# Expert results scattered to token order during the block loop instead of gathered after it, and an attention's first group put ahead of the second batch's rows

## The chip, the cores and the metric

The kernel runs on one core of a Trainium2 chip. Its time is the device time of one execution in microseconds. Engines are named as in the profile: PE (TensorE, matrix products; PEld its weight loads), DVE (VectorE), ACT (ScalarE), POOL (GpSimd), SP (SyncE, which here only issues DMAs; its issues are shown as SPq).

## What is computed

A decoder of four layers on `x` of 4 batches x 512 tokens x 128 features (16 heads), with a context of 77 positions. Every layer is an attention, then a feed-forward part, each with a normalization before and an addition to `x` after.

- Layer 0: causal self-attention with small convolutions, then a mixture of 8 experts (hidden 512, GELU, two experts a token) plus a shared expert.
- Layer 1: attention that samples the context at 5 computed offsets per head, then a mixture of 8 experts with a SiLU gate (hidden 352, two experts a token).
- Layer 2: plain cross attention, then a mixture of 8 experts (hidden 512, ReLU, two experts a token).
- Layer 3: plain cross attention, then product keys: 8192 single-row experts, one chosen per head.

The part that the change touches is the mixture. In the reference:

```python
# layer 0 and 2: every expert, weighted by a gate that is zero but for two experts
for e in range(N_EXPERTS):
    h = act(xf @ Wfc[e] + bfc[e]) @ Wproj[e] + bproj[e]
    routed = routed + h * gate[:, e:e + 1]
# layer 1: rows already multiplied by their gate value and sorted by expert
for e in range(num_experts):
    h = silu(xe @ w1[e]) * (xe @ w3[e])
    out = out + h @ w2[e] * m
```

## The kernel before

**Tiling.** The 2048 tokens are 16 tiles of 128 rows (`NTT`), 4 of them (`NT`) to a batch. `x_all` stays in SBUF for the whole kernel. The kernel is written engine by engine: each stage is a block in which every engine has an own instruction list, and semaphores set what waits for what. So the order on an engine is the order in which the functions of its list are called.

**Stages.** `first_causal` is layer 0's attention and the routing for the first mixture, to about 640 us. Then three times `expert_stage(n)`: the mixture of layer n, and behind it on every engine the attention of layer n+1. Stage 0 is from 640 (sampled attention from 742), stage 1 from 1094 (cross attention from 1194), stage 2 from 1449 (cross attention from 1543, then `product_keys`). The mixture with n == 1 is called `gated`.

**Routing.** Per batch, `normed` (DVE, L649) writes the normalized rows of its four tiles, one operation of 128x128 each. Then logits, the choice of two experts (`pick`) and the number of tokens ahead (`places`) give each row two slots, `slot_i`. `scatter` (POOL, L762) sends each tile's rows twice by indirect DMA to the DRAM array `xs_d`, which is ordered by expert. In the gated layer the rows are multiplied by their two gate values first (`scaled` is the second set of rows).

**Block loop.** The slots are cut into `NBLK` = 23 blocks of `BLK` = 256 rows, each of one expert. For block i: SP loads its rows (L778) into one of three buffers `xb`; PE turns them (`turn`, L956, counted by `m_T`); ACT copies the turned rows out (L1019); PE multiplies up (L974, or L967 and L969 for the two halves of the gated hidden layer); ACT applies the function (L1031 or L1029); in the gated layer DVE multiplies the halves (`gate_hidden`, L877); PE multiplies down (L983, `m_down`); DVE moves the result with its bias to one of two buffers `yb` (`result`, L888, gated L886, counted by `m_y`); SP stores it to `ys_d` (L784), in slot order. DVE also copies the weights of block i+3 (`weights`, L867 to L869, gated L860 to L863). PE's order is `up(i)`, `down(i-1)`, `turn(i+2)`. DVE's order is `gate_hidden(i+1)` (gated only), `result(i)`, `weights(i+3)`. SP's order is `load(i+3)`, `store(i)`.

**Behind the loop.** POOL gathers with two indirect DMAs per tile (L810) the two results of each token from `ys_d`, into four buffers, and waits for the addition of four tiles before. DVE adds them to `x_all` (`combine`; L919 in the gated layer, 128x128 twice a tile; L921 with the gate value otherwise), then computes the attention's statistics (L2525, L2528, in the sampled attention L3096), POOL makes the reciprocal deviations (`rstd`, L2196, L2197), and DVE the normed rows (L2536). In a cross attention PE then turns them (L2264), makes queries (L2270, L2276), products for the rows' maxima (`max_scores`, L2289; DVE's `maxima`, L2543), turns the maxima (L2297; DVE adds them as `maximum_in`, L2557), and per group of four query tiles scores (L2309), exponentials on ACT (L2449) and weighted sums (L2322). The groups are the loop `for G in range(G4)`.

After the loop of stage 1 SP also loads the third mixture's weights (`load_wide`, L212 to L215).

## Time and profile before

| | us |
|---|---|
| three runs | 1899.67, 1910.25, 1910.5 (median 1910.25) |
| profiled execution, its own time | 1902.02 |
| its span | 1900.3 |
| PE busy | 1273.0 (67%) |
| DVE busy | 1026.5 (54%) |
| POOL busy | 565.7 (30%) |
| ACT busy | 530.6 (28%) |

The span is the time from the first to the last recorded instruction; the rest of the execution's time lies around it. The busy shares are means over stages that have different limits, so the views by stage below say more than the table.

### The profile page before, as it was taken

To read this page: it belongs to the slowest core of one execution; us is meant where nothing else is said; L and a number is where in the kernel's file an instruction comes from. 1 tells how busy PE (TensorE), PEld (TensorE's weight loads), DVE (VectorE), ACT (ScalarE), POOL (GpSimd) and SP (SyncE) were. 2 spreads that over 40 slices of the span, in tenths; PEclk is the share of its full clock that TensorE was granted. 3 is DMA by queue.
4 is the path that set the end of the run, shared out by engine and by line. 5 is a ranking of instruction groups with operands and counts; after the bars stand their busy time and mean duration, and the time that the engine had idled before them with its cause. 6 is when DMAs were issued, how large, how long until landed. Compare 5 with 4: busy or idle time off the path is not lost. (4 is left out here: it accounts for less than half of the span.)

```text
span 1900.3 us, 26101 instructions
## 1 busy us (share of the span) xinstructions
PE 1273.0 (67%) x9212; PEld 771.8 (41%) x9212; DVE 1026.5 (54%) x2918; ACT 530.6 (28%) x1053; POOL 565.7 (30%) x700
## 2 busy tenths in 40 slices
PE   1458878787884896455645399378876955787720
PEld 1223334343442785345645288222335842222210
DVE  2454455454553232599999655334433325547796
ACT  0123233332341452122312133023423522323310
POOL 6041222212334002541011600331132033155674
PEclk8588798887995998555555599669967978866665
DMA  5930000000003121433532111400001210022232
GB/s 135 389 136 1 1 1 1 1 1 0 12 7 105 41 67 48 119 100 92 136 93 61 34 60 62 130 23 1 12 18 49 67 49 23 2 63 64 79 98 74
DMA packets 73254, 116.48 MB, mean 61 GB/s; under 512 B 11565, under 2 KB 52320, under 8 KB 70624
## 3 DMA queue, kind: packets, MB, share of 16 engines
q1 hardware_dynamic: 60320, 85.24, 14.9%
q0 software_dynamic: 12800, 29.51, 5.4%
q8 instruction: 76, 1.25, 0.3%
q14 instruction: 58, 0.48, 0.1%
HBM read 77.03 MB, written 37.68 MB: 60 GB/s over the span
## 5 line engine op out<-in xcount | busy, mean ns | idle before, releaser
L1671 DVE CUSTOM_DVE_ANT_0 arena<-ps,far 128x512 f32<-128x512 f32 (+3 forms) x256 | 118.2, 488 | 108.6 <-PE ps L1345 107.7
L2002 POOL DMA_INDIRECT wide<-in_w_ud,arena x128 | 130.0, 1015 | 77.7 <-DVE arena L2033 40.7
L2922 PE MATMUL ps<-wide,arena 78*128 78x32 bf16 x3840 | 112.1, 187 | 51.6 <-ACT wide L3035 41.8
L1260 POOL TENSOR_SCALAR_AFFINE_SELECT arena<-arena 128x260 f32<-128x260 f32 (+1 forms) x128 | 53.7, 432 | 308.9 <-ACT arena L1538 308.8
L810 POOL DMA_INDIRECT arena<-ys_d,slot_i x64 | 61.2, 956 | 246.6 <-DMA ys_d<-arena 197.4
L2922 PEld LDWEIGHTS ps<-wide,arena 78*128 78x128 bf16 x3840 | 110.3, 104 | 58.9 <-ACT wide L3035 45.2
L983 PEld LDWEIGHTS ps<-arena 128*128 128x128 f32 (+1 forms) x1012 | 123.4, 192 | 4.0
L983 PE MATMUL ps<-arena 128*128 128x128 f32 (+1 forms) x1012 | 123.6, 275 | 0.0
L1538 ACT ACTIVATE arena<-ps 128x1024 f32<-128x1024 f32 (+1 forms) x96 | 84.6, 881 | 109.9 <-PE ps L1367 109.4
L1367 PE MATMUL ps<-arena 32*128 32x128 f32 (+3 forms) x512 | 114.2, 491 | 1.1 <-DVE arena L1690 1.1
L2543 DVE TENSOR_REDUCE arena<-ps 128x6 f32<-128x462 f32 (+1 forms) x96 | 54.9, 581 | 93.6 <-PE ps L2289 69.9
L1345 PE MATMUL ps<-fr 32*128 32x256 f32 (+3 forms) x256 | 91.2, 433 | 19.7 <-DVE arena L1671 18.1
L1379 PE MATMUL ps<-arena 128*9 128x128 f32 (+3 forms) x512 | 91.7, 460 | 4.2 <-POOL arena L1260 4.1
L1318 PE MATMUL ps<-arena,wq_rows 128*128 128x512 f32 x96 | 71.9, 910 | 33.5 <-issue 32.5
L2449 ACT ACTIVATE arena<-ps 77x1024 f32<-77x1024 f32 x64 | 65.2, 1019 | 92.7 <-PE ps L2309 75.0
L974 PE MATMUL ps<-arena 128*128 128x256 f32 x368 | 88.6, 384 | 1.6 <-DVE arena L869 1.6
L2322 PE MATMUL ps<-arena 77*9 77x512 f32 x256 | 84.0, 741 | 0.0
L1031 ACT ACTIVATE arena<-ps,arena 128x256 f32<-128x256 f32 x184 | 75.6, 470 | 28.9 <-PE ps L974 28.8
L2309 PE MATMUL ps<-arena 32*77 32x512 f32 x256 | 80.0, 705 | 5.2 <-DVE arena L2557 2.8
L888 DVE TENSOR_TENSOR arena<-ps,b_rows 128x256 f32<-128x256 f32 x46 | 19.5, 424 | 117.9 <-PE ps L983 117.9
L810 POOL DMA_INDIRECT b_rows<-ys_d,slot_i x32 | 38.3, 1198 | 136.4 <-DMA ys_d<-arena 127.3
L1345 PEld LDWEIGHTS ps<-fr 32*128 32x128 f32 x256 | 41.7, 190 | 83.8 <-DVE arena L1671 49.6
(498 smaller groups left out, 2632.4 us busy)
## 6 DMA issues: line engine op xcount, KB each, us to landing
arena<-low_d SPq DMA_DIRECT2D x32, 780.0 KB
xs_d<-zrow SPq DMA_DIRECT2D x1, 10240.0 KB, 30.1
ys_d<-zrow SPq DMA_DIRECT2D x1, 10240.0 KB, 55.9
arena<-xs_d SPq DMA_DIRECT2D x69, 128.0 KB, 2.0
ys_d<-arena SPq DMA_DIRECT2D x69, 128.0 KB, 1.7
arena<-in_w SPq DMA_DIRECT2D x2, 1408.0 KB
wide<-in_Wfc SPq DMA_DIRECT2D x1, 2048.0 KB, 11.8
wide<-in_Wproj SPq DMA_DIRECT2D x8, 256.0 KB, 6.5
```

Of the source, the lines that this page charges most:

```text
L810: pool.indirect_dma_start(out=yg[:, t % 4, j, :], out_offset=None, in_=ys_d, in_offset=bass.IndirectOffsetOnAxis(ap=slot_i[:, j, t:t + 1], ...
L974: nc.tensor.matmul(ps[:, 1 + i % 2 * 2 + c // 2, c % 2 * BLK:c % 2 * BLK + BLK], w1s[:, i % 3, lo:lo + w], xT[:, i % 2, :], start=True, st ...
L983: mm = nc.tensor.matmul(ps[:, 5 + i % 2, t * P:t * P + P], hT[0:w, i % 2, c, t * P:t * P + P], w2s[0:w, i % 3, c, :], start=c == 0, stop=c ...
L1345: mm = nc.tensor.matmul(ps[:, n % 2, 384 * i:384 * i + P * t + P], q3r[rows, G % 2, P * t:P * t + P], kcr[rows, G % 2, 0:P * t + P], start ...
L1367: mm = nc.tensor.matmul(ps[:, 2 + n % 2 * 2 + i, o:o + T - P * kt], kc[rows, G % 3, P * kt:P * kt + P], q3[rows, G % 3, P * kt:T], start=T ...
L1379: mm = nc.tensor.matmul(ps[32 * r:32 * r + HD + 1, 6, P * kt:T], v9[:, G // 4 % 3, kt, 4 * (G % 4) + r, :], pt[:, n // 3 % 2, i, COL[kt]:C ...
L1538: nc.scalar.activation(pt[:, n // 3 % 2, :, o:o + w], ps[:, 2 + n % 2 * 2:4 + n % 2 * 2, 0:w], ACT.Exp, scale=SCALE)\
L1671: ins = nc.vector.tensor_tensor_reduce(junk[:, n % 2, 384 * i:384 * i + w], ps[:, n % 2, 384 * i:384 * i + w], far[:, T - w:T], 1.0, 3 * N ...
L2002: pool.indirect_dma_start(out=rows_g[t % 4][:, h, :], out_offset=None, in_=A["w_ud"], in_offset=bass.IndirectOffsetOnAxis(ap=eidi[:, t % 8 ...
L2309: mm = nc.tensor.matmul(ps[0:S2, 2 + n % 2 * 2 + j, :], kS[rows, G % 4, G // 4, :], q3[rows, G % 3, :], start=True, stop=True)
L2322: mm = nc.tensor.matmul(ps[32 * r:32 * r + HD + 1, 6, :], v9[:, G // 4, 4 * (G % 4) + r, :], pt[:, n % 3, j, :], start=True, stop=True)
L2922: mm = nc.tensor.matmul(ps[:, 2 * (i % 3) + h // 2, col:col + 4 * HD], ring[m_ % 4][:, h * NK + p_, t % 2 * P:t % 2 * P + P], table[n // 4 ...
```

## The change

1. **Rows carry their destination.** `xs_d` gets a 129th column. `normed` writes into it, as a float, the row number in a new array `y_d` where this row's result belongs: token order, one half for first choices and one for second choices. Since a row's two copies now differ, the layers without gates write a second full set of normed rows (`twins`): four operations of 128x128 and two small ones more per batch. In the gated layer `scaled` becomes `twins`, with two small operations more per batch.
2. **Results go to token order.** SP no longer stores. `result(i)` on DVE first computes `goal`, the two addresses of each partition, from column 128 of `xb`, and POOL sends each block's result with two indirect DMAs to `y_d` (`results`). Padding rows go to rows of their own (`trash`).
3. **A load waits for one thing more.** `load(i)` waits not only for the turn of block i-3 but also for `goal` of block i-3, and all loads follow one another on SP.
4. **No gathers.** After the loop SP loads plain rows, two DMAs of 256 KB a batch (`summands`; the last batch's in `last_rows`, with the third mixture's weights behind it in stage 1). `combine` is two additions of 128x512 in the gated layer; in the others still eight operations.
5. **Cross attentions begin in another order.** `maximum_rows(0)`, `queries(2)`, the scores and first weighted sum of group 0 and `maximum_rows(1)` stand ahead of the second batch's rows (`normed(1)`, `rounded_queries(1)`); the loop starts at G = 1.
6. The zero fill of `ys_d` is gone; `load_gated` waits for two scatters.

The core of the diff:

```diff
                 last_user = max((j for j in range(b) if rows[j] is rows[b]), default=-1)
                 if last_user >= 0:
                     dve.wait_ge(scattered[last_user], 32 * NT * (n + 1))
+                nc.vector.tensor_scalar(rows[b][:, :, D], token[:, tiles(b)], float(STAGE * n + NTT * P), None, ALU.add)
+                if not gated:
+                    nc.vector.tensor_scalar(twins[b][:, :, D], token[:, tiles(b)], float(STAGE * n), None, ALU.add)
+                    for t in range(NT):
+                        nc.vector.tensor_scalar(twins[b][:, t, 0:D], xa[:, NT * b + t, :], mv16[:, NT * b + t, 0:1],
+                                                rstd16[:, NT * b + t:NT * b + t + 1], ALU.subtract, ALU.mult)
                 for t in range(NT):
-                    nc.vector.tensor_scalar(rows[b][:, t, :], xa[:, NT * b + t, :], mv16[:, NT * b + t, 0:1],
+                    nc.vector.tensor_scalar(rows[b][:, t, 0:D], xa[:, NT * b + t, :], mv16[:, NT * b + t, 0:1],
                                             rstd16[:, NT * b + t:NT * b + t + 1], ALU.subtract, ALU.mult).then_inc(r["xn"], 1)
...
                     g = lambda j: gval[:, j, ts].unsqueeze(2).to_broadcast([P, NT, D])
-                    nc.vector.tensor_tensor(scaled[b][:, :, :], rows[b][:, :, :], g(0), ALU.mult).then_inc(r["scaled"], 1)
+                    nc.vector.tensor_scalar(twins[b][:, :, D], token[:, ts], float(STAGE * n), None, ALU.add)
+                    nc.vector.tensor_tensor(twins[b][:, :, 0:D], rows[b][:, :, 0:D], g(0), ALU.mult).then_inc(r["scaled"], 1)
                     dve.wait_ge(r["scaled"], 2 * b + 1)
-                    nc.vector.tensor_tensor(rows[b][:, :, :], rows[b][:, :, :], g(1), ALU.mult).then_inc(r["scaled"], 1)
...
+            sent = lambda p, count: 32 * (n * len(range(p, NBLK, 2)) + count)
 
             def sync(sp):
                 def load(i):
                     r = sp.value_load(bmap[0:1, 1, i:i + 1], min_val=0, max_val=SLOTS - BLK)
                     if i >= 3:
                         sp.wait_ge(m["T"], i - 2)
+                        sp.wait_ge(m["goal"], i - 2)
                     sp.dma_start(xb[:, i % 3, :, :], xs_d[bass.ds(r, BLK), :].rearrange("(p c) d -> p c d", c=2))\
                         .then_inc(m[f"x{i % 3}"], 16)
 
-                def store(i):
-                    r = sp.value_load(bmap[0:1, 1, i:i + 1], min_val=0, max_val=SLOTS - BLK)
-                    sp.wait_ge(m["y"], i + 1)
-                    sp.dma_start(ys_d[bass.ds(r, BLK), :].rearrange("(p c) d -> p c d", c=2), yb[:, i % 2, :, :])\
-                        .then_inc(m[f"ys{i % 2}"], 16)
-
                 if n == 0:
+                    for b in (1, 2):
+                        sp.wait_ge(scattered[b], 32 * NT)
                     load_gated(sp)
...
                 sp.wait_ge(m["bmap"], 1)
                 for b in range(B):
                     sp.wait_ge(scattered[b], 32 * NT * (n + 1))
-                for i in range(3):
+                for i in range(NBLK):
                     load(i)
-                for i in range(NBLK):
-                    if i + 3 < NBLK:
-                        load(i + 3)
-                    store(i)
+                settled(sp)
+                for b in range(B - 1):
+                    summands(sp, b)
+
+            def summands(sp, b):
+                if b >= 2:
+                    sp.wait_ge(m["added"], b - 1)
+                for j in range(2):
+                    lo = TRASH + NTT * P * j + T * b
+                    sp.dma_start(yg[b % 2][j], y_d[lo:lo + T, :].rearrange("(t p) d -> p t d", p=P)).then_inc(m[f"ys{b % 2}"], 16)
+
+            def last_rows(sp):
+                summands(sp, B - 1)
                 if n == 1:
                     load_wide(sp, "ffn2", "W1", "W2", "b2")
 
-
-            def gpsimd(pool, rows, scaled):
-                scatter(pool, n, B - 1, rows, scaled)
-
-            def gather(pool, lo, hi):
-                for t in range(lo, hi):
-                    if t >= 4:
-                        pool.wait_ge(m["added"], t - 3)
-                    for j in range(2):
-                        pool.indirect_dma_start(out=yg[:, t % 4, j, :], out_offset=None, in_=ys_d,
-                                                in_offset=bass.IndirectOffsetOnAxis(ap=slot_i[:, j, t:t + 1], axis=0))\
-                            .then_inc(gathered[t % 4], 16)
+            def gpsimd(pool, rows, twins):
+                scatter(pool, n, B - 1, rows, twins)
+
+            def results(pool):
+                for i in range(NBLK):
+                    pool.wait_ge(m["y"], i + 1)
+                    for c in range(2):
+                        pool.indirect_dma_start(out=y_d, in_=yb[:, i % 2, c, :], in_offset=None,
+                                                out_offset=bass.IndirectOffsetOnAxis(ap=goal[:, i % 2, c:c + 1], axis=0))\
+                            .then_inc(landed[i % 2], 16)
 
             def settled(eng):
-                for b in range(2):
-                    eng.wait_ge(m[f"ys{b}"], 16 * len(range(b, NBLK, 2)))
+                for p in range(2):
+                    eng.wait_ge(landed[p], sent(p, len(range(p, NBLK, 2))))
...
                 def result(i, one):
+                    if i >= 2:
+                        dve.wait_ge(landed[i % 2], sent(i % 2, i // 2))
+                    dve.wait_ge(m[f"x{i % 3}"], 16 * (i // 3 + 1))
+                    nc.vector.scalar_tensor_tensor(goal[:, i % 2, :], xb[:, i % 3, :, D], float(-STAGE * n), trash[:, i, :], ALU.add, ALU.max).then_inc(m["goal"], 1)
                     dve.wait_ge(m["down"], i + 1)
-                    if i >= 2:
-                        dve.wait_ge(m[f"ys{i % 2}"], 16 * (i // 2))
                     y = ps[:, 5 + i % 2, 0:BLK].rearrange("p (c d) -> p c d", c=2)
...
             def combine(dve, ch, b):
-                for t in range(NT * b, NT * b + NT):
-                    added_to(dve, ch, t)
-
-            def added_to(dve, ch, t):
-                dve.wait_ge(gathered[t % 4], 32 * (NTT // 4 * n + t // 4 + 1))
+                dve.wait_ge(m[f"ys{b % 2}"], 32 * (b // 2 + 1))
                 for j in range(2):
                     if gated:
-                        ins = nc.vector.tensor_tensor(xa[:, t, :], xa[:, t, :], yg[:, t % 4, j, :], ALU.add)
+                        ins = nc.vector.tensor_tensor(x_all[:, b, :, :], x_all[:, b, :, :], yg[b % 2][j], ALU.add)
                     else:
-                        ins = nc.vector.scalar_tensor_tensor(xa[:, t, :], yg[:, t % 4, j, :], gval[:, j, t:t + 1], xa[:, t, :],
-                                                             ALU.mult, ALU.add)
+                        for t in range(NT):
+                            ins = nc.vector.scalar_tensor_tensor(x_all[:, b, t, :], yg[b % 2][j][:, t, :], gval[:, j, NT * b + t:NT * b + t + 1],
+                                                                 x_all[:, b, t, :], ALU.mult, ALU.add)
                     if j == 0:
...
+                    blocks.results(pool)
...
                 max_scores(0, 0, 12)
+                maximum_rows(0)
+                queries(2)
+                scores(0, 0)
+                scores(0, 1)
+                weighted(0)
+                maximum_rows(1)
                 normed(1)
                 rounded_queries(1)
-                maximum_rows(0)
-                for G in range(G4):
+                max_scores(1, 0, 4)
+                for G in range(1, G4):
                     nb = G // 4 + 1
                     top = lambda n: max_scores(nb, 4 * (G % 4) + n, 4 * (G % 4) + n + 1) if nb < B and G % 4 < 3 else None
                     top(0)
...
                 maxima(0, 0, 12)
                 maximum_out(0)
+                maximum_in(0)
+                maximum_out(1)
                 norms(1)
+                maximum_in(1)
                 normed(1)
-                maximum_in(0)
-                for G in range(G4):
+                maxima(1, 0, 4)
+                for G in range(1, G4):
                     nb = G // 4 + 1
                     more = nb < B and G % 4 < 3
```

DVE in the loop of the gated layer, before. L877 is `gate_hidden` of the next block, L886 the result, L860 to L863 the weight copies.

```order
L877 TENSOR_TENSOR arena<-arena,ps 128x256 [waits m_act] x2
L877 TENSOR_TENSOR arena<-arena,ps 96x256 [waits m_act]
L886 COPY arena<-ps 128x256 [waits m_ys0,m_down]
L855 TENSOR_LOAD bmap
L855 ISA x2
L860 ISA [waits m_down]
L860 COPY arena<-arena 128x352
L861 ISA
L861 COPY arena<-arena 128x352
L862 ISA
L862 COPY arena<-arena 128x256
L863 ISA
```

The same place now. L902 is `gate_hidden`, L909 the new address operation, L913 the result.

```order
L902 TENSOR_TENSOR arena<-arena,ps 128x256 [waits m_act] x2
L902 TENSOR_TENSOR arena<-arena,ps 96x256 [waits m_act]
L909 SCALAR_TENSOR_TENSOR goal<-arena,trash 128x2 [waits m_x2,landed1]
L913 COPY arena<-ps 128x256 [waits m_down]
L880 TENSOR_LOAD bmap
L880 ISA x2
L885 ISA [waits m_down]
L885 COPY arena<-arena 128x352
L886 ISA
L886 COPY arena<-arena 128x352
L887 ISA
L887 COPY arena<-arena 128x256
```

The address operation of a block has come between the gate products of the next block and the result.

SP in the loop of a mixture, before. L778 is the load of a block, L784 the store of a result, L775 and L782 the reading of the block's address.

```order
L775 TENSOR_LOAD bmap
L775 ISA x2
L778 ISA [waits m_T]
L778 DMA arena<-xs_d 128x256
L782 TENSOR_LOAD bmap
L782 ISA x2
L784 ISA [waits m_y]
L784 DMA ys_d<-arena 128x256
```

The same place now. L800 is the load.

```order
L800 DMA arena<-xs_d 128x258
L796 TENSOR_LOAD bmap
L796 ISA x2
L800 ISA [waits m_goal,m_T]
L800 DMA arena<-xs_d 128x258
```

The stores are gone, and each load waits for `m_goal` beside `m_T`.

DVE at the start of the cross attention of stage 1, before. L2551 belongs to the first batch's maxima, L919 are additions of the second batch's results, L2525 to L2536 its statistics and rows, L2557 the maxima's way in for the first group.

```order
L2551 TENSOR_SCALAR arena<-arena 128x16 [waits c_max]
L919 TENSOR_TENSOR x_all<-x_all,arena 128x128 [waits gathered0]
L919 TENSOR_TENSOR x_all<-x_all,arena 128x128 [waits dve_chain]
...
L2525 BN_STATS arena<-x_all 128x6 [waits m_added]
L2525 BN_STATS arena<-x_all 128x6 x3
L2528 BN_AGGR arena<-arena 128x2 [waits c_stats]
L2528 BN_AGGR arena<-arena 128x2 x3
L2536 TENSOR_SCALAR arena<-x_all,arena 128x128 [waits turn7,c_rstd,c_mean]
L2536 TENSOR_SCALAR arena<-x_all,arena 128x128 x3
L2557 TENSOR_TENSOR arena<-arena,ps 128x512 [waits free7_act,turn7]
```

The same place now. L2583 is `maximum_out`, L2589 `maximum_in`, L942 the additions, L2557 to L2568 statistics and rows.

```order
L2583 TENSOR_SCALAR arena<-arena 128x16 [waits c_max]
L2589 TENSOR_TENSOR arena<-arena,ps 128x512 [waits free7_act,turn7]
L2583 TENSOR_SCALAR arena<-arena 128x16 [waits turn7,c_max]
L942 TENSOR_TENSOR x_all<-x_all,arena 128x512 [waits m_ys1]
L942 TENSOR_TENSOR x_all<-x_all,arena 128x512 [waits dve_chain]
L2557 BN_STATS arena<-x_all 128x6 [waits m_added]
L2557 BN_STATS arena<-x_all 128x6 x3
L2560 BN_AGGR arena<-arena 128x2 [waits c_stats]
L2560 BN_AGGR arena<-arena 128x2 x3
L2589 TENSOR_TENSOR arena<-arena,ps 128x512 [waits free7_act,turn7]
L2568 TENSOR_SCALAR arena<-x_all,arena 128x128 [waits turn7,c_rstd,c_mean]
L2568 TENSOR_SCALAR arena<-x_all,arena 128x128 x3
```

The first group's L2589 has moved ahead of the additions and rows of the second batch, and the additions are two.

## Rows read from the trace of the kernel before

**Rows 1.** Busy time by window: PE, PEld, DVE, ACT, POOL, PE clock, DMA
```profile
860.00:1055.00 195.00, 106.28 (x2948) 100.56 (x2946) 185.18 (x340) 45.87 (x137) 34.08 (x27) 0.53 0.36 92
...
1094.00:1194.00 100.00, 98.26 (x598) 87.10 (x598) 56.01 (x172) 36.09 (x93) 0.06 (x1) 0.98 0.19 59
...
1306.00:1316.00 10.00, 6.59 (x30) 2.43 (x28) 7.82 (x33) 3.21 (x4) 1.79 (x4) 1.00 0.00 0
```

**Rows 2.** Timeline of the gated loop: start, duration, operation, idle before
```profile
1158.16 0.38 PE L956 MATMUL ps<-ident,arena 128*128 128x128 f32 x2
...
1161.59 0.42 DVE L877 TENSOR_TENSOR arena<-arena,ps 96x256 f32<-96x256 f32 x1 [0.44 <-ACT arena L1029]
...
1162.31 0.38 PE L956 MATMUL ps<-ident,arena 128*128 128x128 f32 x2
```

**Rows 3.** Timeline of stage 0's loop: PE, DVE and SP
```profile
714.61 0.44 PE L956 MATMUL ps<-ident,arena 128*128 128x128 f32 x2
...
718.71 0.42 DVE L888 TENSOR_TENSOR arena<-ps,b_rows 128x256 f32<-128x256 f32 x1 [2.02 <-PE ps L983]
...
719.31 0.36 SPq L784 DMA_DIRECT2D ys_d<-arena  x1
...
719.96 0.42 DVE L869 COPY arena<-wide 128x512 f32 x1
...
720.42 0.33 SPq L778 DMA_DIRECT2D arena<-xs_d  x1
...
722.45 0.44 PE L956 MATMUL ps<-ident,arena 128*128 128x128 f32 x2
```

**Rows 4.** Timeline, VectorE: normed rows, a small operation
```profile
1417.65 1.20 DVE L649 TENSOR_SCALAR arena<-x_all,mv,rstd 128x128 f32<-128x128 f32 x4 [0.56 <-POOL rstd L640]
...
1229.24 0.18 DVE L2551 TENSOR_SCALAR arena<-arena 128x16 f32<-128x16 f32 x1
```

**Rows 5.** Timeline around indirect DMAs of POOL, and SP's first loads
```profile
1443.71 1.05 POOL L762 DMA_INDIRECT xs_d<-arena,slot_i  x1 [0.30 <-issue]
...
1443.84 0.42 DVE L869 COPY arena<-wide 128x512 f32 x1
...
1446.84 3.65 SPq L778 DMA_DIRECT2D arena<-xs_d  x4
...
817.90 2.15 POOL L810 DMA_INDIRECT b_rows<-ys_d,slot_i  x1 [0.30 <-issue]
```

**Rows 6.** Timeline, ends of the gated and third loops; one DMA group; VectorE addition
```profile
1191.88 0.42 DVE L886 COPY arena<-ps 128x256 f32<-128x256 f32 x1 [0.51 <-PE ps L983]
...
1193.22 0.42 DVE L886 COPY arena<-ps 128x256 f32<-128x256 f32 x1 [0.91 <-PE ps L983]
...
1194.68 12.88 SPq L214 DMA_DIRECT2D wide<-in_W  x8
...
1211.60 0.87 DVE L2525 BATCH_NORM_STATS2 arena<-x_all 128x6 f32<-128x128 f32 x4
...
1542.33 0.43 DVE L888 TENSOR_TENSOR arena<-ps,b_rows 128x256 f32<-128x256 f32 x1 [1.36 <-PE ps L983]
...
1557.09 0.87 DVE L2525 BATCH_NORM_STATS2 arena<-x_all 128x6 f32<-128x128 f32 x4
...
ws<-in_Wproj_s SPq DMA_DIRECT2D x1, 256.0 KB, 4.0
...
1249.20 0.69 DVE L2557 TENSOR_TENSOR arena<-arena,ps 128x512 f32<-128x512 f32 x1 [0.22 <-PE ps L2297]
```

**Rows 7.** Timeline, VectorE: waits behind gathers of later batches
```profile
1274.00 2.99 DVE L2536 TENSOR_SCALAR arena<-x_all,arena 128x128 f32<-128x128 f32 x4 [7.48 <-POOL arena L2197]
...
807.08 0.74 DVE L921 SCALAR_TENSOR_TENSOR x_all<-b_rows,gval,x_all 128x128 f32<-128x128 f32 x2 [4.72 <-DMA b_rows<-ys_d,slot_i]
```

**Rows 8.** Timeline, stage 1's second batch: VectorE additions, TensorE turning rows
```profile
1229.33 2.19 DVE L919 TENSOR_TENSOR x_all<-x_all,arena 128x128 f32<-128x128 f32 x8
...
1234.89 1.23 PE L2264 MATMUL ps<-ident,arena 128*128 128x128 f32 x4 [6.20 <-DVE arena L2536]
```

168 lines of the change are left out of this document (89 added, 79 removed).

## Prediction

> **What bounds the kernel now.** I read the engines' busy time by stage first (the windows), then the timeline of one block in each kind of mixture stage, then the ends of the block loops and the first microseconds of the attentions behind them. The windows say that the three block loops are TensorE's: 98.26 us of matmul in the 100 us from 1094, at a granted clock of 0.98, while the sampled attention from 860 is VectorE's, 185.18 of 195 us [rows 1]. So inside a block loop any wait that TensorE gets is paid in full, and it is paid 20 times over; at the joints between loop and attention, what counts is who comes last. Three places decide the change: the loop of the gated stage, the routing of the rows, and the joints.
>
> **The gated loop (the new wait).** A block's life before: TensorE turns block i (L956) at 1158.16, then multiplies block i-1 up and starts block i-2's down, and turns the next block at 1162.31, a period of 4.15 us [rows 2]. VectorE's last gate product of block i-1 (L877) starts at 1161.59 and takes 0.42, so it ends 3.85 us behind the turn. Before, the load of block i+1 asked only for the turn that had emptied its buffer, three blocks back, and came early. Now it also asks for the address words (`goal`) of block i-2, since these are read from column 128 of the same buffer. On VectorE `goal(i-2)` stands behind the gate products of block i-1 (the first two listings of the change), and these need TensorE's up products of i-1, which stand behind the turn of block i. So each turn now waits for a load that waits for gates that wait for the turn before: one closed ring, whose length is turn to gates 3.85, the address operation 0.2 (the small operation of [rows 4] takes 0.18), from VectorE's end to SyncE's issue 0.18 (copy-out of the other stages: starts 718.71, lasts 0.42, store issued 719.31 [rows 3]), and the load itself 2.03 (issued 720.42, turn at 722.45 in the rows where the turn comes right behind it [rows 3]). The sum is 6.26; with SyncE's small jitter I write 6.28. Against 4.15 that is 2.13 us more, and blocks 3 to 22 have such a load: 20 x 2.13 = **+42.6 us**. The register reads of SyncE (0.75 between two of its issues: 719.31 + 0.36 to 720.42) are done while it waits, and are not in the ring. Nothing hides this: TensorE is what fills the loop. Behind SyncE's wait only the next loads are queued, and TensorE alone waits for those.
>
> **The two loops without gates.** There `goal(i-3)` stands on VectorE behind the result of block i-4 and the weight copies that follow it, with no gates between. The ring is over two blocks: result (L888) at 718.71, end of the last copy 719.96 + 0.42 = 720.38, so 1.67; then 0.2, 0.18 and 2.03, which is 4.08 to the turn; from a turn to the result two products on, 718.71 - 714.61 = 4.10 [rows 3]. Together 8.18, where two blocks now take 722.45 - 714.61 = 7.84. That is 0.17 a block, x 20 x 2 stages = **+6.8**. The first few may have slack, so the bounds are 0 and 10.
>
> **The routing of rows.** `normed` writes in the layers without gates a second set of rows (`twins`): four operations of 128x128, 1.20 us as a group, and two of 128x4, some 0.17 each by the nearest small one [rows 4]: 1.5 per batch. Before the first mixture all four batches lie on VectorE's path or close to it, before the third three to four; take 4 and 3: 10.5. The gated layer gets the two small ones alone, 4 x 0.35 = 1.4. **+11.9**; where VectorE waits for GpSimd's rstd anyway (0.56 before this group) a part may vanish, so 5 to 14.
>
> **Results sent by GpSimd.** Two indirect DMAs per block in place of one store by SyncE. GpSimd is idle during the loops, and an indirect DMA of 128 rows takes it 1.05 with 0.30 between two [rows 5]: 2.7 per block, under the shortest period of 3.9, and landed (1.3 us behind the last: SyncE's first load at 1446.84 less the 0.75 register reads less 1444.76 [rows 5]) before the result two blocks on. Nothing is charged while that holds.
>
> **Joint at the end of a loop.** Gated, before: last results start at 1191.88 and 1193.22, SyncE then issues eight wide loads (12.88 us, 1.6 each), the gathers of the first batch run beside them, and the first batch's statistics start at 1211.60 [rows 6]. Now: the last two pairs by GpSimd from 1192.4, 4 x 1.35 less a gap ends at 1197.5; landed 1198.8; SyncE's two plain loads of 256 KB 0.2 later, 4.0 for the first (a lone one of that size [rows 6]) and 1.6 for the second: 1204.6; two additions of 128x512 at 0.69 [rows 6] behind 0.2: 1206.2. A gain of **5.4**. In the loops without gates, before: last result at 1542.33, statistics at 1557.09 [rows 6]. Now: the last pair starts at 1543.8 (the pair before it holds GpSimd until then) and ends 2.4 later, then 1.3, 0.2, 5.6, 0.2 as above and eight additions of 0.37 (0.74 for two, the operation of the 807.08 row [rows 7]), 3.0: 1556.5. A gain of 0.6 each, **1.2**. The zero fill of the old result array is not on the path and counts nothing.
>
> **Joints between batches.** The gathers of the second half stand on GpSimd ahead of the third batch's rstd; VectorE waits 7.48 us there (1274.00), and the next stage repeats the pattern; in the sampled attention the adds themselves wait 4.72 (807.08) [rows 7]. With plain loads issued early by SyncE these go: 7.0 + 7.0 + 4.7 = **18.7**. Late next is then GpSimd's rstd itself, for which I leave the remainder. Two additions for eight in the gated combine: 2.19 [rows 8] to 1.4; one batch of the three stands on the path, **0.8**.
>
> **The first group ahead of the second batch's rows.** TensorE stands 6.20 us before 1234.89, waiting for the rows of batch 1 [rows 8]. The change puts maximum rows, queries and scores of that group into this hole. Scores need ScalarE's exponentials behind them, and batch 1's rows come later by them, so I grant 2.5 us of the 6.2 in the first such attention and 1.0 in the second, where VectorE's eight additions stay: **3.5**, with bounds from -2 to 6.
>
> **Sum.** 42.6 + 6.8 + 11.9 = 61.3 lost; 5.4 + 1.2 + 18.7 + 0.8 + 3.5 = 29.6 won; net +31.7. The profiled execution took 1902.0 us (span 1900.3), so 1933.7 on its scale; by the median of the runs shown, 1910.25, 1942. Three runs are at 1910.25, 1910.5 and 1899.67; the profiled one lies low among them, and I predict between the two, **1938**.
>
> **Rivals.**
> A. The clock. With 4.15 us of matmul in 6.28, TensorE would be busy for 66% of the gated loop. The sampled attention shows 106.28 of 195 us busy at a clock of 0.53; against it, ten microseconds at 6.59 busy from 1306 had 1.00 [rows 1]. If it falls to the lower level (1.2 GHz), the part of the ring that is matmul, some 2.8 us, doubles: 20 x 2.8 = 56 more, 1993. 10%.
> B. GpSimd's scatters are held up, and the wait for landed results takes over as the ring. For it: one indirect DMA took 2.15 (817.90) beside long VectorE operations; against it, 1.05 beside the copies of the block's weights, 0.42 at 1443.84 [rows 5]. Two of 2.15 are 4.3, 0.34 above the period without gates; x 40 = 14 more, 1951. 8%.
> The Trainium skill ("SBUF — State Buffer", section "SBUF: two separate sides", its warning on VectorE and DMA) says that a DMA issued by GpSimd stalls while VectorE copies fp32 within SBUF, since both want one port pair; the weight copies of each block are of that kind. By that rule each pair of scatters would grow by up to the block's copies, 1.0 to 1.2 us, which alone would still fit into either period. The trace speaks against even that much: the 1.05 row stands beside such copies.
> C. The other side: the gated load's wait is hidden, because the address operation comes a block earlier than I read. Then +42.6 falls away: 1938 - 43 = 1895, about 1885 with a bigger gain at the joints, which is faster. It decides where the load lands before TensorE is ready to turn, so where `goal` ends 2.2 us (issue and landing) ahead of the turn. The gates end at 1162.01, only 0.30 ahead of the turn at 1162.31 [rows 2], so it takes a `goal` of one block before, whose gates ended 4.15 earlier. The order speaks against it. 10%, for what I may have misread there.
> D. The gains at the joints don't come, since GpSimd's rstd, or the first loads, are late instead: only 10 of 29.6. 1938 + 20 = 1958. 7%.
>
> **How the numbers follow.** Forecast 65%, own range 1920 to 1955 (routing 5 to 14, gateless loops 0 to 10, first group -2 to 6, plus the two scales 8 apart). The range reaches over B and D, and a little down: **1915 to 1958**; outside lie A and C, 20%. One per cent (1891 to 1929) is about what a measurement of this kernel can tell from no change. Faster: half of C and a trace of the forecast, 0.06; same: the other half of C and the low end of the forecast, 0.10; slower: 0.84.
>
> **What would show it.** In the profile of the changed kernel: a period of 6.3 us between turns in the gated loop, TensorE idle some 2 us before each turn with the load as its releaser, and the loop about 43 us longer; 4.1 in the other two; each load issued 0.2 behind a `goal`; no 7 us wait before the third batch's normed rows; the clock still near 1 in the gated loop. I am wrong if the load of block i+1 is seen to be issued before the gates of block i-1 end, if the clock there is near 0.5, or if the scatters of a block take longer than its period.

## The result, and the profile after

The changed kernel takes 1961.72 us (median of four runs, 1957.04 to 1965.78), the kernel before 1904.97 (1899.67 to 1910.5): a ratio of 1.0297, with an interval of 1.0247 to 1.0346. It is 57 us slower. The forecast was slower too, by 32 us: 1938, with a range to 1958, and the time lies 4 us above that range. The profiled executions have spans of 1900.3 and 1955.3, so there are 55.0 us to be found between the two traces.

To find them I cut both timelines at the same nine events: first turn of each block loop, last result of it, first statistics of the attention behind it. The three of the gated stage in the changed kernel, in rows like those in [rows 2] and [rows 6] (start, duration, operation, idle before):

```profile
1103.98 0.66 PE L980 MATMUL ps<-ident,arena 128*128 128x128 f32 x2 [4.67 <-DMA arena<-xs_d]
...
1254.11 0.43 DVE L913 COPY arena<-ps 128x256 f32<-128x256 f32 x1 [0.85 <-PE ps L1007]
...
1264.65 0.87 DVE L2557 BATCH_NORM_STATS2 arena<-x_all 128x6 f32<-128x128 f32 x4
```

All stretches, each from the event before to the one named:

| stretch, to | before | after | difference | forecast |
|---|---|---|---|---|
| first turn of stage 0 | 647.0 | 660.4 | +13.4 | +6.0 |
| last result of stage 0 | 93.0 | 98.0 | +4.9 | +3.4 |
| first statistics behind it | 14.6 | 13.1 | -1.6 | -0.6 |
| first turn of stage 1 (sampled attention) | 339.3 | 332.5 | -6.8 | -3.3 |
| last result of stage 1 (gated loop) | 99.3 | 150.1 | +50.9 | +42.6 |
| first statistics | 18.4 | 10.5 | -7.8 | -5.4 |
| first turn of stage 2 (cross attention) | 237.4 | 237.2 | -0.2 | -5.8 |
| last result of stage 2 | 93.3 | 97.9 | +4.6 | +3.4 |
| first statistics | 14.8 | 11.1 | -3.7 | -0.6 |
| end (cross attention, product keys) | 343.2 | 344.5 | +1.3 | -8.0 |
| sum | 1900.3 | 1955.3 | +55.0 | +31.7 |

**The ring is there.** Two blocks of the gated loop after, where [rows 2] had a turn every 4.15 us (a row of PE L980 is a turn, L902 is the gate product, L909 the addresses):

```profile
1162.36 0.44 PE L980 MATMUL ps<-ident,arena 128*128 128x128 f32 x2 [1.91 <-DMA arena<-xs_d]
...
1165.84 0.42 DVE L902 TENSOR_TENSOR arena<-arena,ps 96x256 f32<-96x256 f32 x1 [0.44 <-ACT arena L1053]
1166.17 0.15 DVE L909 SCALAR_TENSOR_TENSOR goal<-arena,trash 128x2 int32<-128x2 f32 x1
...
1168.51 0.44 PE L980 MATMUL ps<-ident,arena 128*128 128x128 f32 x2 [1.79 <-DMA arena<-xs_d]
1168.73 0.96 POOL L835 DMA_INDIRECT y_d<-arena,goal  x1 [0.30 <-issue]
1168.78 0.89 PE L991 MATMUL ps<-arena 128*128 128x256 f32 x2
1169.47 1.06 PE L993 MATMUL ps<-arena 128*128 128x256 f32 x2
```

TensorE now stands idle before each turn, 1.8 to 2.0 us (once 2.2), and it is the load that releases it. From turn to gate end to addresses to the next turn are 6.15 us, where 6.28 had been worked out. But look at the last two rows: the same pair of up products that took 0.59 us now takes 0.89 and 1.06. The next turn comes at 1176.45, 7.94 behind. Of the 20 periods with a waiting load, 14 are 6.1 to 6.3 and six are 7.8 to 8.3. The granted clock falls to 0.5 in this loop six times, for 3.41 us each, and the six long periods are those.

**The joints are shorter**, and by more than forecast. The end of the gated loop, to compare with [rows 6]:

```profile
1253.47 0.96 POOL L835 DMA_INDIRECT y_d<-arena,goal  x1 [1.71 <-DVE arena L913]
...
1257.27 0.96 POOL L835 DMA_INDIRECT y_d<-arena,goal  x1 [0.30 <-issue]
1259.53 6.03 SPq L821 DMA_DIRECT2D arena<-y_d  x6
1263.20 1.42 DVE L942 TENSOR_TENSOR x_all<-x_all,arena 128x512 f32<-128x512 f32 x2 [8.66 <-DMA arena<-y_d]
```

Between SyncE's first load and the additions lie 3.7 us; I had 5.8 for them, made of 4.0 for a lone transfer, 1.6 for the second and 0.2 behind it. The 4.0 of [rows 6] isn't a lone transfer's: it was issued 0.47 us behind another of 256 KB, in a row of loads issued one behind the other:

```profile
36.54 0.43 SPq L233 DMA_DIRECT2D ws<-in_Wfc_s  x1
37.01 0.43 SPq L233 DMA_DIRECT2D ws<-in_Wproj_s  x1
```

The first of these took 3.6 us to land, the second 4.0, so both were there 4.5 us behind the first issue. The company was in that figure already, and the 1.6 charged it once more.

**The clock in the last cross attention** is the third thing to see. Windows of 20 us from the first statistics of stage 2 (length, busy PE, PEld, DVE, ACT, POOL with the number of instructions, PE clock, DMA share and GB/s):

```profile
1610.80:1630.80 20.00, 13.17 (x28) 6.00 (x28) 10.88 (x31) 2.35 (x4) 2.53 (x3) 0.67 0.09 26
1630.80:1650.80 20.00, 13.56 (x34) 4.42 (x33) 7.62 (x24) 4.28 (x6) 2.53 (x3) 0.59 0.09 27
1650.80:1670.80 20.00, 17.16 (x46) 5.14 (x44) 8.61 (x29) 5.84 (x7) 1.29 (x3) 0.67 0.00 0
1670.80:1690.80 20.00, 16.80 (x38) 4.79 (x39) 4.79 (x9) 4.38 (x6) 3.46 (x2) 0.50 0.00 1
```

TensorE is busy for 16.80 of 20 us in the last of them, and gets little done: 38 products, since it runs at 1.2 GHz throughout.

### The profile page after: what moved, and what is told of

The parts are those of the page before. It is cut to its first block and busy times, and to the rows that moved or that the text cites. A ratio compares the mean times of both kernels' runs of the same rounds, so it can differ in the third digit from the quotient of the medians.

```text
span 1955.3 us, 25917 instructions
## 1 busy us (share of the span) xinstructions
PE 1326.0 (68%) x9212; PEld 788.1 (40%) x9212; DVE 1049.0 (54%) x3019; ACT 531.6 (27%) x1053; POOL 599.5 (31%) x744
## 5 line engine op out<-in xcount | busy, mean ns | idle before, releaser
L835 POOL DMA_INDIRECT y_d<-arena,goal x138 | 133.0, 964 | 255.5 <-DVE arena L915 130.9
L2953 PE MATMUL ps<-wide,arena 78*128 78x32 bf16 x3840 | 109.9, 187 | 50.0 <-ACT wide L3066 41.5
L1392 PE MATMUL ps<-arena 32*128 32x128 f32 (+3 forms) x512 | 121.0, 522 | 1.2 <-DVE arena L1715 1.2
L1370 PE MATMUL ps<-fr 32*128 32x256 f32 (+3 forms) x256 | 92.4, 439 | 18.1 <-DVE arena L1696 16.5
L1404 PE MATMUL ps<-arena 128*9 128x128 f32 (+3 forms) x512 | 99.0, 492 | 1.4 <-POOL arena L1285 1.4
L1343 PE MATMUL ps<-arena,wq_rows 128*128 128x512 f32 x96 | 70.0, 888 | 31.7 <-issue 30.7
L2349 PE MATMUL ps<-arena 77*9 77x512 f32 x256 | 89.0, 782 | 2.2 <-ACT arena L2479 2.2
L2336 PE MATMUL ps<-arena 32*77 32x512 f32 x256 | 86.1, 787 | 4.9 <-DVE arena L2589 4.9
L980 PE MATMUL ps<-ident,arena 128*128 128x128 f32 x138 | 30.8, 308 | 62.7 <-DMA arena<-xs_d 60.9
## 6 DMA issues: line engine op xcount, KB each, us to landing
wide<-in_Wfc SPq DMA_DIRECT2D x1, 2048.0 KB, 11.1
```

Of the source, the lines that this page charges most:

```text
L835: pool.indirect_dma_start(out=y_d, in_=yb[:, i % 2, c, :], in_offset=None, out_offset=bass.IndirectOffsetOnAxis(ap=goal[:, i % 2, c:c + 1] ...
L1370: mm = nc.tensor.matmul(ps[:, n % 2, 384 * i:384 * i + P * t + P], q3r[rows, G % 2, P * t:P * t + P], kcr[rows, G % 2, 0:P * t + P], start ...
L1392: mm = nc.tensor.matmul(ps[:, 2 + n % 2 * 2 + i, o:o + T - P * kt], kc[rows, G % 3, P * kt:P * kt + P], q3[rows, G % 3, P * kt:T], start=T ...
L1404: mm = nc.tensor.matmul(ps[32 * r:32 * r + HD + 1, 6, P * kt:T], v9[:, G // 4 % 3, kt, 4 * (G % 4) + r, :], pt[:, n // 3 % 2, i, COL[kt]:C ...
L2336: mm = nc.tensor.matmul(ps[0:S2, 2 + n % 2 * 2 + j, :], kS[rows, G % 4, G // 4, :], q3[rows, G % 3, :], start=True, stop=True)
L2349: mm = nc.tensor.matmul(ps[32 * r:32 * r + HD + 1, 6, :], v9[:, G // 4, 4 * (G % 4) + r, :], pt[:, n % 3, j, :], start=True, stop=True)
```

## The experiments

The questions were: is the gated loop the ring of load and gates, and what are its six long periods; why does the start cost 13.4; and why do the two cross attentions give back nothing. All ratios below are to the kernel before, run on the same chip.

**e1: addresses one block earlier.** Four address buffers, and the operation ahead of the gate products:

```diff
+                def address(i):
+                    if i >= 4:
+                        dve.wait_ge(landed[i % 2], sent(i % 2, i // 2 - 1))
+                    dve.wait_ge(m[f"x{i % 3}"], 16 * (i // 3 + 1))
+                    nc.vector.scalar_tensor_tensor(goal[:, i % 4, :], ...)
+
                 def result(i, one):
+                    dve.wait_ge(m["down"], i + 1)
                     if i >= 2:
                         dve.wait_ge(landed[i % 2], sent(i % 2, i // 2))
-                    dve.wait_ge(m[f"x{i % 3}"], 16 * (i // 3 + 1))
-                    nc.vector.scalar_tensor_tensor(goal[:, i % 2, :], ...)
-                    dve.wait_ge(m["down"], i + 1)
...
+                address(0)
...
                 for i in range(NBLK):
+                    if i + 1 < NBLK:
+                        address(i + 1)
                     if gated and i + 1 < NBLK:
                         gate_hidden(i + 1)
```

> The changed kernel with four address buffers, and the addresses of block i+1 computed ahead of the gate products of block i+1 (one block earlier than now), everything else as changed. Ring theory: the load of a block no longer stands behind the gates, turns in the gated loop come every 4.15 to 4.3 us with no longer one in between, the first turn to the last result takes 100 us where it now takes 150, and the loops without gates win some 4 us each: 1961.7 - 51 - 8 = about 1903. Rival, that the 23 pairs of indirect DMAs (or the wait for what they have landed) hold the loops: periods stay above 5 us and the time above 1940.

Measured: 1879.18 us (1875.57 to 1880.14), ratio 0.9855 (0.9833 to 0.9877). The gated loop takes 98.5 us (150.1 in the changed kernel, 99.3 before); its periods, but for the first two, are 4.14 to 4.16. Two turns a block apart, and between them the address operation, now well ahead of the load that asks for it:

```profile
1143.77 0.39 PE L987 MATMUL ps<-ident,arena 128*128 128x128 f32 x2
...
1145.78 0.15 DVE L909 SCALAR_TENSOR_TENSOR goal<-arena,trash 128x2 int32<-128x2 f32 x1
...
1147.92 0.38 PE L987 MATMUL ps<-ident,arena 128*128 128x128 f32 x2
```

So the ring was the cause of the loop's growth, and the 23 pairs of scatters are no bound. The whole kernel came out 24 us better than I expected. The loops without gates are the largest part of that: 88.0 and 89.0 us where I expected 94. Their period is 3.73 from the fourth at the latest, which is shorter than before the change (93.0; pairs like 3.79 and 4.2).

**e2: the old order of the cross attentions**, on all engines, with everything else as changed. TensorE's part:

```diff
                 max_scores(0, 0, 12)
-                maximum_rows(0)
-                queries(2)
-                scores(0, 0)
-                scores(0, 1)
-                weighted(0)
-                maximum_rows(1)
                 normed(1)
                 rounded_queries(1)
-                max_scores(1, 0, 4)
-                for G in range(1, G4):
+                maximum_rows(0)
+                for G in range(G4):
```

> The changed kernel with both cross attentions in the order of before (first group behind the second batch's rows). As predicted (the new order wins 3.5 us): 1965. Rival, that the new order costs, since the first group's products run before TensorE's clock has risen and push the second batch's rows back: 1952 to 1958, and the third batch's normed rows start at or under 59 us behind the first statistics of stage 1, where the changed kernel has 60.8.

Measured: 1943.83 us (1941.9 to 1946.12), ratio 1.0199 (1.0177 to 1.022): 18 us less than the changed kernel, more than the rival had said. It is not in stage 1 (236.9 against 237.2; the third batch's normed rows start 60.3 behind the first statistics, not under 59) but in the last stretch: 330.4 against 344.5. The windows that answer to those above:

```profile
1611.50:1631.50 20.00, 10.70 (x22) 4.75 (x22) 12.10 (x36) 2.34 (x4) 2.53 (x3) 0.67 0.09 26
1631.50:1651.50 20.00, 14.56 (x46) 5.76 (x47) 7.23 (x22) 5.99 (x8) 2.53 (x3) 0.77 0.09 27
1651.50:1671.50 20.00, 14.54 (x53) 5.49 (x53) 11.78 (x34) 4.82 (x6) 4.75 (x4) 0.83 0.00 0
1671.50:1691.50 20.00, 18.11 (x73) 5.76 (x73) 6.55 (x15) 9.20 (x12) 0.00 (x0) 1.00 0.00 1
```

With the new order TensorE does more in the first 20 us (28 products against 22), as intended. From then on its clock is lower: 0.59, 0.67, 0.50 against 0.77, 0.83, 1.00, and after 80 us the old order has done 194 products to the new one's 146.

**e3 and e7: idle products in the wait.** 12, then 8 products of 128x128 that nobody reads, on TensorE ahead of each turn in the gated loop.

```diff
+                    if gated and i and i + 2 < NBLK:
+                        pe.wait_ge(m["xT"], i + 1)
+                        for _ in range(12):
+                            nc.tensor.matmul(ps[:, 7 * (i % 2), 3 * P:4 * P], ident[:, :], ident[:, :], start=True, stop=True)
```

> The changed kernel with 12 idle products of 128x128 put on TensorE ahead of each turn of the gated loop, 1.5 us that should fit in its wait of 1.8 to 1.95. Clock theory (every third block runs 1.65 us longer because the clock falls to 1.2 GHz after TensorE's waits): all periods 6.2 to 6.3, granted clock 1.0 over the loop, 7 x 1.65 = 11.6 us less: 1950. Rival (the long blocks come from late loads or from GpSimd): one period of 7.9 in three stays, and the time is 1962 or more.

Measured: 1958.16 us (1950.16 to 1960.21), ratio 1.026 (1.0229 to 1.029). All periods but one (7.51) are 6.83 to 6.88, none is 7.9, the clock is 1.0 from 1110.2 on, and the loop takes 152.7. The 12 products take 2.84 us, more than the wait. The size was wrong, so the test said little about the price. With 8:

> The changed kernel with 8 idle products ahead of each turn of the gated loop instead of 12 (12 took 2.84 us and were longer than the wait). Clock theory: 8 take 1.9 us and fit, all periods 6.2 to 6.3 with a granted clock of 1.0, first turn to last result 139 to 141 instead of 150, time 1950. Rival (the late third period has another cause): periods of 7.9 stay.

Measured: 1947.93 us (1944.65 to 1951.51), ratio 1.0233 (1.0202 to 1.0265). Every waiting period is 6.15 to 6.64, the loop takes 140.7. (The 8 products show as x16.)

```profile
1152.35 0.15 DVE L909 SCALAR_TENSOR_TENSOR goal<-arena,trash 128x2 int32<-128x2 f32 x1
1152.71 0.33 SPq L800 DMA_DIRECT2D arena<-xs_d  x1
1152.73 1.95 PE L1023 MATMUL ps<-ident 128*128 128x128 f32 x16
...
1154.82 0.44 PE L980 MATMUL ps<-ident,arena 128*128 128x128 f32 x2
1155.10 0.60 PE L991 MATMUL ps<-arena 128*128 128x256 f32 x2
```

And the two loops in one window each, of the changed kernel and then of this one:

```profile
1104.00:1254.00 150.00, 111.62 (x598) 94.13 (x598) 62.34 (x194) 36.25 (x93) 40.96 (x44) 0.92 0.13 39
```

```profile
1106.00:1246.00 140.00, 136.74 (x917) 122.40 (x916) 62.35 (x194) 36.16 (x93) 40.55 (x43) 0.99 0.14 41
```

The waits are still there, filled. What has gone is the clock's fall: it is 1.0 from 1109.3 to the loop's end, and the loop is 9.4 us shorter. So the 50.9 us of the gated loop are 41.5 of the ring (99.3 to 140.7; forecast 42.6) and 9.4 of the clock that the ring's waits cost.

**e4: without the second set of rows** in the layers without gates. This kernel leaves out what the mixtures of layers 0 and 2 give; ahead of the first loop it computes what the changed kernel does.

```diff
-                if not gated:
-                    nc.vector.tensor_scalar(twins[b][:, :, D], ...)
-                    for t in range(NT):
-                        nc.vector.tensor_scalar(twins[b][:, t, 0:D], ...)
...
-                    src = (twins if j == 0 else rows)[b]
+                    src = (twins if gated and j == 0 else rows)[b]
```

> The changed kernel without the second set of normed rows in the layers without gates: both copies of a row come from one set, the results of these two layers all go to the padding rows, and the additions read those, so the layers' outputs are left out; the number and size of all DMAs stay. Sum of the prediction (1.4 per batch, 7 to 8 batches): 10 less, 1952. Rival, that the 13.4 us lost ahead of the first block loop are these operations together with the clock that they cost TensorE: first turn near 647 to 649 instead of 660, 1945. Second rival, that these operations lie beside other work: less than 4 us, 1958 or more.

Measured: 1941.11 us (1940.01 to 1944.04), ratio 1.0188 (1.0167 to 1.0209): 21 us less than the changed kernel. The first turn is at 643.0, so the second set costs 17.4 us ahead of the first loop alone, for three to four batches of 1.5 us. Followed along the first attention (starts of GpSimd's selections, times of the kernel before), the distance to the kernel before is about -4 from the second batch on and stays there; in the changed kernel it goes from +0.7 to +5.7 between 492 and 503, to +8.2 by 526 and to +13.8 by 566. Windows there, of the kernel before and of the changed one:

```profile
490.00:500.00 10.00, 9.50 (x53) 4.26 (x50) 3.88 (x16) 3.43 (x5) 7.04 (x11) 1.00 0.11 34
...
570.00:580.00 10.00, 5.00 (x24) 2.91 (x24) 1.97 (x6) 0.70 (x2) 4.38 (x6) 0.63 0.08 27
```

```profile
490.00:500.00 10.00, 10.00 (x34) 3.94 (x31) 2.43 (x13) 2.84 (x4) 4.97 (x8) 0.50 0.09 28
...
570.00:580.00 10.00, 10.00 (x34) 3.42 (x32) 0.00 (x0) 3.41 (x5) 3.66 (x6) 0.50 0.05 15
```

In the first window TensorE is busy without a gap and at half its clock, where before it had the full one; in the second the clock of the kernel before has begun to fall too. The steps stand where the granted clock is at 0.5 in the changed kernel: from 489.7 to 503.4, 523.8 to 530.7 and 568.2 to 588.7. In the kernel before and in e4 it is 1.0 from about 480 to 572.7 and from 476 to 568.4. e1, e2, e3, e5 and e7 have the same code ahead of the first loop, show falls at the same places, and have their first turns at 659.0 to 663.0, while the three kernels with the code of before (before, e8, e9) have them at 647.0 to 649.1. A fall and a step go together elsewhere too: e6 and e8 have a single fall of 6.8 us, at 518.8 and 517.6, and with it a single step of 2.4 and 2.5. The operations themselves are a few microseconds; the rest goes with the clock. e4 takes away the operations and the falls together, and no run restored the clock alone, so that the falls are what the steps cost is read from the rows.

**e5: early addresses and the old order**, the edits of e1 and e2 together.

> Addresses one block earlier, and both cross attentions in the order of before. If the two causes add up: 1879 less the 14.1 us that the old order saved behind the first statistics of stage 2: 1865, the last stretch (first statistics of stage 2 to the end) 330 us. Rival, that the 14 us were a chance of where that run's clock stood and not of the order: 1879 again, last stretch 340 or more.

Measured: 1874.75 us (1864.23 to 1875.17), ratio 0.9832 (0.9793 to 0.9872). That is 4 us less than e1, and the intervals of the two ratios overlap. The last stretch is 333.3 (339.9 in e1), near the 330 that the theory wanted, but stage 1's attention is 239.3 (235.4 in e1), and the time is 10 us over the 1865 expected. The two causes don't simply add up. Three of the four runs lie within 0.8 us and the fourth 10 us below them, so one kernel has differences of that size between its own executions.

**e6: the second set copied by ScalarE**, on top of e5.

```diff
+                if not gated:
+                    act.wait_ge(r["xn"], NT * b + NT)
+                    nc.scalar.copy(twins[b][:, :, 0:D], rows[b][:, :, 0:D]).then_inc(r["twin"], 1)
```

> As the kernel with early addresses and the old order, but ScalarE copies the second set of normed rows (one copy of 128x512 per batch) in place of VectorE's four operations. Theory (the second set costs its 17 us ahead of the first loop because VectorE keeps TensorE waiting at the end of a group and the clock falls): first turn at 643 to 650 instead of 660, time 1846 to 1855. Rival (ScalarE is as much in the way, or the address columns alone do it): first turn at 658 or more, time 1865.

Measured: 1857.28 us (1848.51 to 1864.56), ratio 0.9763 (0.9715 to 0.9811), the fastest kernel of the study, 17 us under e5. The first turn is at 651.1, 7.9 us earlier than e5's and one later than the theory's window; e4's 643.0 isn't reached. Two early periods of the first loop are then 5.54 and 4.67, so that 5.3 us of the 7.9 are left at its end. The other gain I had not expected: stage 1's attention takes 226.7 us, where e5 has 239.3. TensorE's instructions in it are the same and in the same order in both, and the third batch's statistics come 57.0 us behind the first ones in e5 and 48.3 in e6, before either kernel does any routing there. This is one profiled execution of each, and the four runs of e6 alone spread over 16 us: whether the kernels differ here or only the two executions, is open. Windows of 20 us from 20 us behind the first statistics, of e5, then e6:

```profile
1219.90:1239.90 20.00, 16.30 (x39) 6.18 (x39) 5.65 (x15) 5.66 (x7) 1.26 (x2) 0.59 0.86 262
1239.90:1259.90 20.00, 19.81 (x46) 5.77 (x44) 7.87 (x24) 4.82 (x6) 1.51 (x3) 0.50 0.00 1
```

```profile
1213.50:1233.50 20.00, 14.24 (x47) 5.67 (x48) 8.05 (x24) 7.26 (x9) 1.26 (x2) 0.79 0.86 262
1233.50:1253.50 20.00, 15.44 (x57) 5.53 (x55) 10.72 (x28) 5.34 (x7) 3.48 (x3) 0.83 0.00 1
```

In both the clock is low for 13.7 us from some 15 us behind the first statistics. Then e5's falls again 3.4 us later and stays low for 41.0 us, where e6's stays up for 23.9.

**e8: only the new order, in the kernel before**, the edit of e2 backwards.

> The kernel before, with gathers and stores as they were, and only the new order of the cross attentions. If the order by itself costs: 10 to 20 us more than the kernel before, 1916 to 1925, most of it behind the first statistics of stage 2. As predicted (it wins 3.5): 1902.

Measured: 1916.02 us (1907.87 to 1921.44), ratio 1.0059 (1.0035 to 1.0082): 11 us more. The stretch behind the first statistics of stage 2 grows by 7.9 (343.2 to 351.2), that of stage 1 by 2.2. The order costs by itself, some half of what it does in the changed kernel.

**e9: stores of the kernel before by GpSimd**, so that SyncE's list holds only loads.

```diff
+            def stores(pool):
+                pool.wait_ge(m["bmap"], 1)
+                for i in range(NBLK):
+                    r = pool.value_load(bmap[0:1, 1, i:i + 1], min_val=0, max_val=SLOTS - BLK)
+                    pool.wait_ge(m["y"], i + 1)
+                    pool.dma_start(ys_d[bass.ds(r, BLK), :].rearrange("(p c) d -> p c d", c=2), yb[:, i % 2, :, :])\
+                        .then_inc(stored[i % 2], 16)
```

> The kernel before, with the stores of the block results issued by GpSimd (plain DMAs) in place of SyncE, so that no load stands behind a store on SyncE. Early addresses had the gateless loops at 88 us and a period of 3.73, where the kernel before has 93 and pairs of 3.8 and 4.1. Theory, that this comes from SyncE's order alone: gateless loops at 88 to 89, the gated one unchanged near 98.5, time 1904.6 - 10 = 1895. Rival, that it comes from something else in the changed kernel: loops stay at 93, time 1902 to 1907.

Measured: 1900.55 us (1888.96 to 1905.02), ratio 0.9976 (0.9951 to 1.0). The loops do what the theory says: 88.0, 98.2 and 89.7 us where the kernel before has 93.0, 99.3 and 93.3. That is 9.7 us won in the loops, and the time is the same: in its profiled execution, stage 1's attention takes 247.0 instead of 237.4. The joints behind the three loops are longer too, by 4.2 us in all, and the last stretch is 4.1 shorter. The gain is there and is given back later in this execution, the slowest of its ten; the median run is 1.2 us under the kernel before, with an interval that ends at no gain. Why stage 1's attention takes more I can't show; e5 and e6 show that this stretch takes 12 us more or less with equal TensorE instructions. What held the gateless loops of the kernel before is shown: SyncE stood in front of the store of one block (18 times, 32.2 us in the first loop), with the next load behind it.

**e10: e6 with the new order**, that is the edits of e1 and e6 without that of e2.

> Early addresses, the second set copied by ScalarE, and the new order of the cross attentions (the kernel of e6 has the old). If the new order costs here too: stretch behind the first statistics of stage 2 some 7 to 14 longer than 330, time 1861 to 1871. If its cost hangs on where the clock stands and may be none: within 3 us of 1857.

Measured: 1868.0 us (1856.97 to 1877.87), ratio 0.9811 (0.9752 to 0.9871). The last stretch is 336.5 (330.1 in e6), stage 1's attention 238.9 (226.7). Its single runs overlap with e6's, so the time alone would not decide; with e2 and e8 the last stretch has been 14, 8, 7 and 6 us longer with the new order in four pairs out of four (e2, e8, e1 against e5, e10 against e6). All twelve traces sort themselves by the order of that attention, in every column (times behind its first statistics):

| | clock from 20 to 80 us | third batch's statistics | last stretch |
|---|---|---|---|
| gathers, old order: before, e9 | 0.81, 0.79 | 49.9, 51.5 | 343.2, 339.1 |
| gathers, new order: e8 | 0.59 | 57.6 | 351.2 |
| no gathers, old order: e2, e5, e6 | 0.87, 0.76, 0.87 | 49.4, 53.9, 48.9 | 330.4, 333.3, 330.1 |
| no gathers, new order: changed, e1, e3, e4, e7, e10 | 0.56 to 0.62 | 57.1 to 60.0 | 336.5 to 347.0 |

In stage 1's attention they don't: its times are 226.7 to 247.0 with the old order and 234.5 to 239.6 with the new.

## Why the prediction was wrong

**The gated loop: mechanism right, term too small.** "One closed ring" of turn, gates, address, load stood there as written, and e7 shows it in one period of 6.15 to 6.64 us after the other, for the 6.28 worked out; e1 takes it away and with it 51.6 us. What the step left out is in the sentence "Nothing hides this: TensorE is what fills the loop". A wait of TensorE costs twice: the wait, and then the products behind it when the clock has fallen. It was rival A, in a form I hadn't thought of. I had the clock either stay up or fall for the whole loop (56 us more). It fell in six periods of 20, for 3.41 us each, which made them some 1.7 us longer; e7 measures the whole at 9.4 us.

**The gateless loops: small, and right in kind.** 4.9 and 4.6 in place of 3.4 each. The pairs sum mostly to 8.3 to 8.4 where I had 8.18. I left out one thing. Before, the loads had stood behind the stores on SyncE; without stores and without the ring, the period is 3.73 and not 3.92 (e9, e1), and this gain, 5.0 and 3.6 us in e9, the change would have had. The ring takes it and 4.9 and 4.6 us more.

**The routing of rows: mis-sized, and by e4 the term furthest off at one place.** I took "four operations of 128x128, 1.20 us as a group", times the number of batches on the path: 6.0 ahead of the first loop. The stretch grew by 13.4, and e4 puts the second set at 17.4, since 4 us were won there by something else (not known; the zero fill of the old result array is work that the change takes away there, and was not tested by itself). The step that failed is the price of an operation as its own duration: with the four operations more the clock is at 0.50 in whole windows where it was at 1.00. The bound of 5 to 14 for the whole term held only operations and no consequence of them.

**The gathers: right.** The waits of [rows 7] are gone: the third batch's normed rows now wait 0.52 for GpSimd where it was 7.48. Without gathers and with the old order the last stretch takes 330.1 to 333.3 us (e2, e5, e6), with gathers 343.2 and 339.1 (before, e9): 6 to 13 less, where I gave it 7.0. In stage 1's attention e2, with the second set's operations still in it, came out even with the kernel before. The sampled attention gained 6.8 where 3.3 were forecast. The joints gained 13.1 in all where 6.6 were: the two plain loads took 3.7 us and not 5.8, since I had read the row of 4.0 as a lone transfer's.

**The first group ahead of the second batch's rows: wrong in sign.** The step said: "TensorE stands 6.20 us before 1234.89, waiting for the rows of batch 1 [rows 8]. The change puts maximum rows, queries and scores of that group into this hole", and granted 3.5 us, bounds -2 to 6. The hole was filled: the first exponentials in the last attention come 22.3 us behind the first statistics, not 30.9. But the products that had stood among the second batch's maxima, and had kept TensorE busy while VectorE reduced, were the ones taken away. What is left there is a chain of single products, each waiting for VectorE's reduction:

```profile
1641.57 0.75 PE L2316 MATMUL ps<-fr 128*128 128x462 f32 x1 [0.68 <-ACT fr L2468]
1643.05 0.76 PE L2316 MATMUL ps<-fr 128*128 128x462 f32 x1 [0.73 <-DVE arena L2575]
1644.54 0.62 PE L2316 MATMUL ps<-fr 128*128 128x308 f32 x1 [0.73 <-DVE arena L2575]
1645.73 0.75 PE L2316 MATMUL ps<-fr 128*128 128x462 f32 x1 [0.57 <-DVE arena L2575]
```

With the old order (e2) scores (L2336) and weighted sums (L2349) stand between the same products:

```profile
1643.48 0.41 PE L2316 MATMUL ps<-fr 128*128 128x308 f32 x1 [0.73 <-DVE arena L2570]
1643.82 1.08 PE L2336 MATMUL ps<-arena 32*77 32x512 f32 x4
1644.84 1.03 PE L2349 MATMUL ps<-arena 77*9 77x512 f32 x4
1645.80 0.48 PE L2316 MATMUL ps<-fr 128*128 128x462 f32 x1
```

The chain of the new order runs at the lower clock (0.75 us for a product that takes 0.48 here), and so does what follows. The third batch's statistics come 57.2 us behind the first ones with the new order and 49.4 with the old, the fourth's 107.4 and 92.4. A gain of 8.6 for the first group became a loss of 15 for the fourth batch. That the order costs is shown (e2, e8 and the table in e10); that the maxima's chain is what holds the clock down is read from the rows, and no run here changed only that.

**Rival B** (scatters held up) did not happen: 138 indirect DMAs at a mean of 0.96 us, though each pair runs beside the weight copies of its block. The Trainium skill ("SBUF — State Buffer", section "SBUF: two separate sides") warns that a DMA issued by GpSimd stalls beside such copies; in this loop the DMAs show no sign of it. VectorE does: the weight copy of 128x256 that runs beside a scatter takes 0.47 us, where the same copy took 0.29 (at 1155.19) in the kernel before. In the gated loop it is off the ring and costs nothing. In the loops without gates the copies are on the ring, and there the second one of 128x512 takes 0.63 to 0.65 in place of 0.42 in 18 blocks of the 23 of the first loop, which is about as much as the pairs are over 8.18. (My price for this rival was too low besides: two of 2.15 with the 0.30 between are 4.9 us, not 4.3.) The group of the scatters, and such a copy beside the first scatter of a pair, in the changed kernel:

```profile
L835 POOL DMA_INDIRECT y_d<-arena,goal x138 | 133.0, 964 | 255.5 <-DVE arena L915 130.9
```

```profile
1126.79 0.96 POOL L835 DMA_INDIRECT y_d<-arena,goal  x1 [4.03 <-DVE arena L913]
...
1127.37 0.47 DVE L887 COPY arena<-arena 128x256 f32 x1
```

**Rivals C and D** did not happen as written. D's outcome (the gains don't come) did in the two cross attentions, through the clock and not through GpSimd's rstd.

In sum, on the profiled spans: forecast 31.7; start +7.4, gated loop +8.3, gateless loops +2.7, joints -6.5, sampled attention -3.5, cross attentions +14.9, together 23.3, which gives 55.0. The joints and the sampled attention came out 10.0 better than forecast, the one by a misread row and the other for no reason that I can show; without this luck the miss would have been 33 us. The chance for slower, 0.84, was well placed. The step that failed throughout is that a wait, an operation or a moved product was priced by its own duration. The range was too narrow since it took each term's bounds from the durations of operations and left the clock to one all-or-nothing rival.

## What to carry to other kernels

- When a buffer's release is tied to one more reader, look where that reader stands in its engine's order. Here a 0.15 us operation behind the gate products closed a ring that cost 51 us. One block earlier it cost nothing, and the kernel was 1.4% faster than the one before (e1), with the second set copied by ScalarE and the old order 2.4% (e6).
- In a stage where TensorE runs in short pieces between waits, price a new wait or a moved product at the clock it may cost, and give the range that spread. Two kernels with equal TensorE lists differed by 12.6 us in one attention of this program, by one trace each. So compare a stretch over several traces before you put a few microseconds of it down to an edit.
- A filling of a hole is worth what remains behind it: ask which products kept the engine busy where they stood before.
